# A token's two expert weights stored in its row and gathered with it, and the x2 stores and parked weights of an attention and mixture-of-experts kernel requested later

## The reference

```python
x = x + layernorm(attention(layernorm(x)))   # 16 heads of 16, rotary embedding, Wo
x = x + layernorm(moe(layernorm(x)))
```

```python
d2 = sum(xs*xs) + sum(centroid*centroid) - 2*(xs @ centroid.T)
w, sel = top_k(sqrt(max(d2, 1e-12)), 2)
w = softmax(w)                                # the token's two weights
out = sum over the two chosen e of
      w_e * ((silu(xs @ Wg[e] + bg[e]) * (xs @ W1[e] + b1[e])) @ W2[e] + b2[e])
```

## Time and profile before

| | |
|---|---|
| median of 3 runs | 1604.24 us |
| lowest, highest | 1593.34, 1605.25 us |
| profiled execution | 1608.56 us, its span 1605.8 us |
| PE, PEld busy | 1377.3 us (86%), 876.6 us (55%) |
| DVE busy | 1116.9 us (70%) |
| ACT busy | 958.9 us (60%) |
| POOL busy | 629.6 us (39%) |

### The profile page before, as it was taken

One profiled execution on the slowest core, in us unless ns is written; L12 is line 12 of the kernel. 1 busy time (PEld: TensorE's weight loads), 2 busy tenths in 40 slices (PEclk: granted clock), 3 DMA queues, 4 the chain that ended last, 5 costly groups with the idle time before them and its releaser, 6 DMA issues.

```text
span 1605.8 us, 31875 instructions
## 1 busy us (share of the span) xinstructions
PE 1377.3 (86%) x10413; PEld 876.6 (55%) x10414; DVE 1116.9 (70%) x1890; ACT 958.9 (60%) x1755; POOL 629.6 (39%) x464
## 2 busy tenths in 40 slices
PE   7899999999999999999998439888888888888860
PEld 5454433343333334343454228878878888778860
DVE  6998999999999999995045675455445544554444
ACT  4523888888888878888734324444444444444435
POOL 4750033121313222224123044555555555555545
PEclk9998999999999999999968759999999999999995
DMA  6985357566565646650467714444444444444556
GB/s 210 268 217 101 89 116 184 167 175 187 88 185 92 152 66 155 97 117 12 126 116 198 283 69 140 120 106 111 119 120 110 107 120 120 110 109 118 161 143 209
DMA packets 181488, 220.39 MB, mean 137 GB/s; under 512 B 57583, under 2 KB 152748, under 8 KB 178837
## 3 DMA queue, kind: packets, MB, share of 16 engines
q1 hardware_dynamic: 165493, 200.52, 47.0%
q0 software_dynamic: 15904, 18.66, 6.6%
HBM read 146.64 MB, written 72.48 MB: 136 GB/s over the span
## 4 chain that ended last, share of the span: by engine, by line
DVE 38%; PE 28%; DMA 16%; issue 13%; POOL 2%; ACT 1%; DVEq 1%; SPq 0%; POOLq 0%; ACTq 0%
DVE mx L1094 25%; DMA w_slot<-w_d,at_w 13%; PE psum L1707 4%; PE psum L1680 4%; DVE psum L1087 3%; PE psum L1871 3%; PE psum L1694 2%; DVE h_lo L1327 2%; PE psum L1781 2%; PE psum L1852 2%; PE psum L1854 2%; PE psum L1853 2%; PE psum L1640 2%; DMA y_d<-values,at_y 2%; PE psum L1654 2%
## 5 line engine op out<-in xcount | busy, mean ns | idle before, releaser
L1478 ACT ACTIVATE work<-psum 128x512 f32<-128x512 f32 x1024 | 543.7, 600 | 93.7 <-PE psum L1694 69.0
L1094 DVE TENSOR_REDUCE mx<-psum 128x1 f32<-128x1024 f32 (+1 forms) x512 | 546.8, 1097 | 24.4 <-PE psum L1680 11.1
L1680 PE MATMUL psum<-stack 48*128 48x512 f32 x1024 | 377.4, 450 | 21.3 <-DVE mx L1094 10.9
L1694 PE MATMUL psum<-stack 50*128 50x512 f32 x1024 | 375.8, 451 | 0.0
L1680 PEld LDWEIGHTS psum<-stack 48*128 48x128 f32 x1024 | 162.1, 187 | 262.2 <-DVE mx L1094 169.0
L1707 PE MATMUL psum<-work,values 128*32 128x384 f32 x4080 | 304.4, 394 | 0.2
L955 POOL DMA_INDIRECT values<-xn_d,at_x x71 | 149.1, 2100 | 221.6 <-DVE at_w L1344 208.1
L1317 DVE COPY small<-w_slot 128x1 f32 (+1 forms) x71 | 10.9, 154 | 266.9 <-DMA w_slot<-w_d,at_w 266.9
L1852 PE MATMUL psum<-w_hi,x_hi 128*128 x568 | 188.7, 332 | 1.8 <-DVE x_lo L1312 1.0
L1853 PE MATMUL psum<-w_lo,x_hi 128*128 x568 | 182.3, 321 | 0.0
L1854 PE MATMUL psum<-w_hi,x_lo 128*128 x568 | 182.2, 321 | 0.0
(11 more groups left out here) (201 smaller groups left out, 2059.4 us busy)
## 6 DMA issues: line engine op xcount, KB each, us to landing
stack<-qk_scr SPq DMA_DIRECT2D x192, 128.0 KB, 6.1
work<-in_w SPq DMA_DIRECT2D x36, 640.0 KB
small<-in_w SPq DMA_DIRECT2D x35, 640.0 KB
qk_scr<-weights SPq DMA_DIRECT2D x16, 1024.0 KB, 4.7
split_raw<-in_w SPq DMA_DIRECT2D x8, 1368.0 KB
wh_d<-w_hi SPq DMA_DIRECT2D x6, 1368.0 KB, 5.8
w_hi<-wh_d SPq DMA_DIRECT2D x6, 1368.0 KB, 13.0
ot_scr<-weights SPq DMA_DIRECT2D x16, 512.0 KB, 3.2
```

The source lines that it names most:

```text
L1094: dve.tensor_reduce(mx[:, r, a, t:t + 1], scored, AX, ALU.max, negate=True).then_inc(s_max, 1)
L1478: act.activation(pt[u % 4][:, j, :], bank((c + HG * u + n) % 3), ACT.Exp, scale=SC).then_inc(s_exp, 1)
L1680: ins = pe.matmul(bank(4 + 2 * a + half), qs[t3][at:at + QROWS, r, P * t:P * (t + 1)], ks[t3][at:at + QROWS, r, 512 * half:512 * (half + 1 ...
L1694: pe.matmul(bank((t3 + HG * u + n) % 3), ks[t3][at:at + MROWS, r, P * st:P * (st + 1)], qs[t3][at:at + MROWS, r, 512 * half:512 * (half + ...
```

## The change

Each row of `xn2_d` becomes two numbers longer (258 instead of 256). The two weights of a token are stored there by one DMA from `w_pair` (128 partitions x 32 x 2), issued by SP behind the wait for the x2 stores and before `load_high(4)`. The gather of a row brings them along in `x_row` (258 columns). A table `choice` (two numbers for each slot: 1 and 0 for a first choice, 0 and 1 for a second, as place is below 4096 or not) is made with two DVE operations at the end of the routing. In each tile DVE multiplies the two gathered numbers by the slot's pair (`pick_weight`) and adds the two products (`keep_weight`), with `aim_gather` between them.

Left out are `w_d` with its zeros, the transpose of the weights on PE, the copy on ACT and the store of it, and in each tile `gather_weight` on POOL with `aim_weight` on DVE.

In the batch stage `store_x2` of all units is moved behind u = 8, and `load_high(0)` and `load_high(1)` to u = 12 and 14.

```diff
-        w_both = sb("w_both", [P, 2, NT])
-        w_slot = sb("w_slot", [P, 1])
+        choice = dots_sb[:, 27:, :]...[:, 0:2 * NS].rearrange("p (s a) -> p s a", a=2)
+        w_pair = sb("w_pair", [P, NT, 2])
+        w_1, w_2 = w_pair[:, :, 0], w_pair[:, :, 1]
+        w_slot = sb("w_slot", [P, 2])
...
-        x_row = [c.take([C]) for _ in range(2)]
+        x_row = [c.take([C + 2]) for _ in range(2)]
-        xn2_d = nc.dram_tensor("xn2_d", (NTOK, C), F32, kind="Internal").ap()
+        xn2_d = nc.dram_tensor("xn2_d", (NTOK, C + 2), F32, kind="Internal").ap()
-        w_d = nc.dram_tensor("w_d", (2 * NTOK + P, 1), F32, kind="Internal").ap()
...
-            sp.wait_ge(s_zero, 1)
-            sp.dma_start(w_d[2 * NTOK:, :].rearrange("(a n) o -> a (n o)", a=1), zeros[0:1, 0:P]).then_inc(s_wd, 16)
...
-                if u % 2 == 1:
-                    store_x2(u // 2)
-                if u in (2, 3):
-                    load_high(sp, u - 2)
+                for m in {8: (0, 1), 9: (2, 3), 10: (4,), 11: (5,), 13: (6,), 15: (7,)}.get(u, ()):
+                    store_x2(m)
+                if u in (12, 14):
+                    load_high(sp, u // 2 - 6)
...
             sp.wait_ge(s_x2s, 16 * (NT // 4))
+            sp.wait_ge(s_w12, 1)
+            sp.dma_start(xn2_d.rearrange("(n p) c -> p n c", p=P)[:, :, C:], w_pair[:, :, :]).then_inc(s_wd, 16)
             for e in range(4, E - 1):
                 load_high(sp, e)
-            sp.wait_ge(s_wc, 1)
-            sp.dma_start(w_d[0:2 * NTOK, :].rearrange("(a p) o -> a (p o)", p=P), w_turned).then_inc(s_wd, 16)
-            sp.wait_ge(s_wd, 32)
...
-            def gather_weight(t):
-                pool.wait_ge(s_iw, t + 1)
-                after(pool, s_wk, t)
-                settle(pool, passed_pool)
-                pool.indirect_dma_start(out=w_slot[:, :], out_offset=None, in_=w_d, ...).then_inc(s_wg, 16)
...
+            step(dve.tensor_scalar(choice[:, :, 0], place_of[:, :], float(NTOK), None, ALU.is_lt))
+            step(dve.tensor_scalar(choice[:, :, 1], place_of[:, :], float(NTOK), None, ALU.is_ge))
...
+            def pick_weight(t, p):
+                after(dve, s_wk, 2 * t)
+                dve.tensor_tensor(w_slot[:, :], x_row[p][:, C:C + 2], choice[:, bass.ds(t, 1), :]...,
+                                  ALU.mult).then_inc(s_wk, 1)
+
             def keep_weight(t):
-                dve.wait_ge(s_wg, 16 * (t + 1))
-                dve.tensor_copy(w_all[:, bass.ds(t, 1)], w_slot[:, :]).then_inc(s_wk, 1)
+                dve.wait_ge(s_wk, 2 * t + 1)
+                dve.tensor_tensor(w_all[:, bass.ds(t, 1)], w_slot[:, 0:1], w_slot[:, 1:2], ALU.add).then_inc(s_wk, 1)
...
                     low_x(t + 1)
-                    keep_weight(t + 1)
+                    pick_weight(t + 1, 1 - p)
                 if not isinstance(t, int) or t + 3 < NS:
                     aim_gather(t + 3, 1 - p)
-                if not isinstance(t, int) or t + 2 < NS:
-                    aim_weight(t + 2)
+                if not isinstance(t, int) or t + 1 < NS:
+                    keep_weight(t + 1)
...
-            act.wait_ge(s_wt, 1)
-            act.activation(w_turned, bank(6)[0:2 * NT, 0:P], ACT.Copy).then_inc(s_wc, 1)
...
-                act.wait_ge(s_wk, t + 1)
+                act.wait_ge(s_wk, 2 * t + 2)
...
-            pe.wait_ge(s_w12, 1)
-            pe.transpose(bank(6)[0:2 * NT, 0:P], w_both[:, :, :].rearrange("p a n -> p (a n)"), ident[:, :]).then_inc(s_wt, 1)
```

More of the change, by code:

```diff
@@ L271, in build @@
         cent_t = sb("cent_t", [P, KC, 32])
-        w_both = sb("w_both", [P, 2, NT])
-        w_1, w_2 = w_both[:, 0, :], w_both[:, 1, :]
-        w_slot = sb("w_slot", [P, 1])
+        choice = dots_sb[:, 27:, :].rearrange("p n c -> p (n c)")[:, 0:2 * NS].rearrange("p (s a) -> p s a", a=2)
+        w_pair = sb("w_pair", [P, NT, 2])
+        w_1, w_2 = w_pair[:, :, 0], w_pair[:, :, 1]
+        w_slot = sb("w_slot", [P, 2])
         row_of = sb("row_of", [P, NS])
-        at_w = sb("at_w", [P, 1], I32)
         token_of = sb("token_of", [P, NS])
@@ L397, in build @@
         s_w12 = sem("weights_of_choices_ready")
-        s_wt = sem("weights_of_choices_turned")
-        s_wc = sem("weights_of_choices_copied")
         s_wd = sem("weights_of_choices_stored")
-        s_iw = sem("weight_gather_aimed")
-        s_wg = sem("slot_weights_gathered")
-        s_wk = sem("slot_weights_kept")
+        s_wk = sem("slot_weight_step")
         s_bh = sem("slot_tiles_compared")
@@ L982, in _ @@
                 pool.wait_ge(kept_of, 16 * NT // 8)
-            pool.wait_ge(s_wd, 32)
+            pool.wait_ge(s_wd, 16)
             def tile(t, p):
@@ L1313, in low_x @@
                                   x_hi[:, :, :].rearrange("p k t -> p (k t)").bitcast(F32), ALU.subtract).then_inc(s_mx, 1)
+            def pick_weight(t, p):
+                after(dve, s_wk, 2 * t)
+                dve.tensor_tensor(w_slot[:, :], x_row[p][:, C:C + 2], choice[:, bass.ds(t, 1), :].rearrange("p s a -> p (s a)"),
+                                  ALU.mult).then_inc(s_wk, 1)
             def keep_weight(t):
-                dve.wait_ge(s_wg, 16 * (t + 1))
-                dve.tensor_copy(w_all[:, bass.ds(t, 1)], w_slot[:, :]).then_inc(s_wk, 1)
+                dve.wait_ge(s_wk, 2 * t + 1)
+                dve.tensor_tensor(w_all[:, bass.ds(t, 1)], w_slot[:, 0:1], w_slot[:, 1:2], ALU.add).then_inc(s_wk, 1)
             def multiply(t, c):
@@ L1340, in aim_scatter @@
                 dve.tensor_copy(at_y[:, :], row_of[:, bass.ds(t, 1)]).then_inc(s_is, 1)
-            def aim_weight(t):
-                after(dve, s_wg, 16 * t)
-                dve.tensor_copy(at_w[:, :], place_of[:, bass.ds(t, 1)]).then_inc(s_iw, 1)
             def tile(t, p):
@@ L1369, in _ @@
             aim_gather(1, 1)
-            aim_weight(0)
             low_x(0)
+            pick_weight(0, 0)
+            aim_gather(2, 0)
             keep_weight(0)
-            aim_gather(2, 0)
-            aim_weight(1)
             for t in range(4):
```

6 lines of the change are left out of this document (removed).

## The result

The changed kernel takes 1495.8 us (median of 4 runs, 1490.3 to 1500.8) beside 1603.1 us of the kernel before: 0.934 of its time (95% interval 0.928 to 0.939), 107 us less. On two other chips it took 1482.1 us beside 1612.4 (0.923, 0.918 to 0.928) and 1478.2 us beside 1603.6 (0.926, 0.921 to 0.930), 130 and 125 us less. Both sizes, 107 and about 128, have to be explained.

A forecast was written before the change was run, and what follows sets the result against it. The prediction took PE's bubble behind DVE's wait for gathered weights as the bound in the tiles. Tiles -98.9, batch stage -9.8 and routing +0.5 sum to -108.2 us, giving 1496 us, range 1480 to 1545.

The forecast's parts named there:

- What bounds the kernel: Expert tiles: DVE waits 3.9 us a tile for gathered weights, costing PE about 1.6 us idle; price the latter.
- PE's 6.79 us: Expert tiles: PE's undisturbed time per tile, 3.98 us from gate_up to down plus 2.81 to the next gate_up.
- the division by a clock of 0.99: Expert tiles: the granted clock averaged 0.99, which made PE's 6.79 us a tile into 6.86.
- The tiles under x2's loads: Last tiles: they keep their length, two at 9.04 us and one at 8.4, 26.5 us.
- DVE's spare time: Expert tiles: h_lo ready at +3.55 us, PE wants it at +4.7, so 1.2 us to spare.
- The scatters' round: Expert tiles: 5.16 us to landing plus 1.40 to the next scatter, 6.56 us, 0.30 below PE's.
- the rival that had 0.26: Expert tiles: scatters set the pace if landing exceeds 5.46 us, kernel 1512 at 5.7, 1544 at 6.2; chance 0.26.
- The denser traffic: Expert tiles: the same 3.9 us of DMA time in shorter tiles, 56% up from 45%; could delay scatter landings.
- Rows of 1032 bytes: Gathers in the tiles: five or six transactions a row instead of four, reads up by up to a half, hidden.
- The batch stage: Batch 3's inverses land sooner: POOL gains 5.9 us, unit 12 at full clock 4.0; together 9.8 us less.
- The routing: Two operations for choice add 0.5 us; the 8-byte store of pairs, at most 13.8 us, is hidden in idle time.
- The total: Whole kernel: -98.9 - 9.8 + 0.5 = -108.2 us, median 1604.24 to 1496.

The follow-up runs named there:

- e3_wait_moved: Kernel before with both gathers kept; DVE's weight copy and aim moved behind low_hidden, POOL's weight gather ahead of the scatter: 1501.3 us beside 1602.4 (0.938).
- e2_batch_only: Kernel before with only the x2 stores and the two loads of parked weights moved in the batch stage: 1589.9 us (0.994).
- e9_extra_small: Changed kernel plus a DRAM-to-DRAM copy of 512 rows (0.5 MB) behind every tile's second-layer weights: 1479.0 us in one run.
- e1_tiles_only: Changed kernel with the x2 stores and the two parked-weight loads back at their old places in the batch stage: 1496.1 us (0.934).
- e6_tiles_again: Changed kernel with x2 stores and two parked-weight loads at their old places, measured on another chip: 1495.6 us beside 1482.1 of the changed kernel.

## Why the prediction was right, and where not

- **What bounds the kernel.** Right. PE's bubble was the price, not DVE's wait: over 68 tiles the mean fell by 1.57 us, from 8.40 to 6.83; the bubble had been 1.6, DVE's wait 3.9. `e3_wait_moved` shows it from the other side: the wait gone from its place, the gather kept, the same time.
- **PE's 6.79 us.** Right, from two rows of before. Only the division by a clock of 0.99 was too much: the other 65 tiles took (464.6 - 24.1) / 65 = 6.78 us, 5.4 us less in all. The tiles under x2's loads took 24.1 us, not 26.5. Together the tiles gave 106.7 us, not 98.9.
- **DVE's spare time.** Foretold 1.2 us, found 1.18.
- **The scatters' round.** This term was mis-sized. I took 5.16 us to landing from one row of the chain. The chain shows a landing only where it came last, so it picks long ones. The trace of before gives no other landings; in `e2_batch_only`, whose tiles are those of before, the one landing that the chain has within the tiles is 4.9 us, the longest of all, and the median is 3.9. It is 3.8 in after. The 1.40 us behind the landing came from one round too. With 1.13 from landing to start the round is 4.9 us, not 6.56, and the rival that had 0.26 was never near. Since it wasn't on the path, the forecast didn't suffer, only the chances and the upper end of the range.
- **The denser traffic** (DMA share 0.46 before and 0.57 after, 955 to 1400 us) did not make a landing longer. `e9_extra_small` moved another 0.5 MB a tile, share 0.78, and then it did: 5.5 us.
- **Rows of 1032 bytes.** The gathers land in 2.8 us (median), the aligned rows of 1 KB in `e2_batch_only` and `e3_wait_moved` in 4.2. Most of this difference is the hold on POOL that the last section describes: from the end of the instruction (0.99 us long, against 2.01 and 2.21) it is 1.8 us against 2.2 and 2.0. So the gathers show no cost. The Trainium skill's rule for them ("DMA: Bandwidth & Descriptors", "How a descriptor splits into AXI transactions") was worked out wrongly: such a row starts a multiple of 8 bytes behind a boundary (if the table itself starts at one) and always takes five transactions, so the reads grow by up to a quarter, not a half. A cost does show in another place, which the prediction overlooked: the store of ones into `xn2_d` ahead of the stage, 4096 pieces of 512 bytes. It landed in 13.8 to 13.9 us in the three kernels with rows of 1024 bytes and in 19.7 to 22.6 us in the eleven with rows of 1032, while the store of zeros to `y_d`, which the change leaves alone, took 13.9 to 14.4 in all. It was hidden under the attention stage.
- **The batch stage.** Right, and in both terms: -9.8 foretold, 9.7 less from `norm_o` of batch 2 to the routing (65.4 to 55.7). By the unrounded starts 5.9 of them lie ahead of `norm_o` of batch 3 (foretold 5.9) and 3.9 behind it, where the clock stayed at 1.00 (foretold 4.0). Which request was to blame was left open and is settled now: the loads.
- **The routing.** +0.5 foretold and found (48.6 to 49.1). Pieces of 8 bytes landed in 7.2 us (7.2 to 9.0 in the eleven traces that have them), within the bound of 13.8, and were hidden. The same page's "Specifications" has pieces below 512 B need a read-modify-write; if it cost anything here, 4096 pieces of 8 bytes still took about half of what 4096 pieces of 512 took, and per byte over 30 times more.
- **The total.** -108.2 foretold and -107.8 found in the two spans, but partly by chance. The tiles gave 7.8 us more than I said, and the clock took 8.2: 21.7 lost from 100 to 175 us, 13.5 won from 797 to 828. The change by itself is worth some 115 us, by the three lines of the table. The medians of the two other chips, 125 and 130 us apart, hold some 10 to 15 us on top of it, about one low stretch of the clock: on the third chip four of six runs of the changed kernel are of its upper level, and the lowest runs of the two kernels are 115.8 us apart there (on the second chip 125.0, where no run of before had a mean clock above 0.951). That before had the low stretch in most of its runs fits this and isn't shown. The 14 us between executions of one kernel were missing from my working: I looked for the clock only where the change was.

## What to carry to other kernels

An engine's wait costs what the engine behind it loses; follow it to the bounding engine's bubble and price that (1.6 us here, not 3.9). Before a DMA is taken out, look whether its wait can stand elsewhere: in `e3_wait_moved` a copy moved behind three other operations of DVE, with the gather one place forward on POOL, gained as much as the gather's removal. A short wait of the bounding engine can cost more than its length, when the clock falls behind it (8.7 us for a wait of 2.5). When the length of a row changes, look at every DMA that writes or reads it, also at those far from the change. Take a duration for a rival from the median of a group (landings of a line), never from the chain, which picks the late ones; and when two kernels differ by less than 1%, compare the granted clock by stretch before the medians.

## What the runs showed of the hardware

**TensorE's granted clock falls while PE is fully busy, in some executions only.** In all 14 traces PE idles 0.76 or 0.77 us ahead of the first `project_o` (before: at 795.27). In seven, before among them, the clock is 0.50 from about 2 us later for some 31 us, with PE busy all the time, and this costs 13.5 to 14.3 us (44.7 us to `norm_o` of batch 2 against 30.4 to 31.2). In seven it stays at 1.00. It starts ahead of every moved request and belongs to no kernel: the same code had it in `e1_tiles_only` and not in `e6_tiles_again`. It is also what the two levels of the changed kernel's times look like: on the second and third chip the runs of 1476 to 1482 us have mean clocks of 0.951 to 0.958, those of 1491 to 1494 us 0.934 to 0.947. Where the low stretch lay in runs that were not profiled isn't shown. A stretch at 0.50 as long as that at the start of after (100 to 175 us) appeared in one trace of 14. What lets the clock fall in either place stays open.

**The gather on POOL is held up while `low_w2` runs on DVE.** With its start within `low_w2`, a gather ended 0.86 us after `low_w2` did: by the earlier trace rows `low_w2` ends at 1188.10 + 1.76 = 1189.86, and the gather of before's trace at 1188.72 + 2.00 = 1190.72. So it is in 68 of before's 71 gathers (0.82 to 0.87 us), whatever their own length. In `e3_wait_moved` it is the same 0.86 with a gather of 2.36 us. In after 64 gathers start up to 0.42 us ahead of `low_w2` (median 0.31) and take 0.99 us. A gather of after, then that of `e3_wait_moved`:

```profile
1150.60 1.00 POOL L946 DMA_INDIRECT values<-xn_d,at_x  x1 [0.30 <-issue]
```

```profile
1152.69 2.36 POOL L955 DMA_INDIRECT values<-xn_d,at_x  x1 [0.30 <-issue]
```

So part of before's loop over the gather of weights, which stands behind this gather on POOL, was 1.0 us of such holding (2.00 against 0.99). The Trainium skill, "SBUF — State Buffer", section "Who interferes with whom", says that a DVE instruction with two SBUF inputs contends with a GpSimd instruction that reads SBUF, and that who comes first keeps the port pair; `low_w2` has both inputs in SBUF, and these rows agree in both orders, if a gather counts as such an instruction; its indices lie there, but which part of it waits isn't shown.
